# Eight edge counts of the next graph's near mask half, placed at other steps of the attention slot

## The reference

```python
h = jnp.maximum(_layernorm(x), 0.0)
x = x + _L0_gnn_ref(adj, h, W, b)      # max over the first 25 neighbours, then relu(concat(h, agg) @ W + b)
h = jnp.maximum(_layernorm(x), 0.0)
x = x + _L1_gnn_ref(h, adj, ...)       # attention, then feed-forward, each with residual and layer norm

# inside _L1_gnn_ref
allowed = (adj > 0) | (jnp.swapaxes(adj, 1, 2) > 0) | eye
scores = jnp.einsum('bhqd,bhkd->bhqk', q * scale, k)        # 8 heads of 16
scores = jnp.where(allowed[:, None], scores, -jnp.inf)
ctx = jnp.einsum('bhqk,bhkd->bhqd', softmax(scores), v)
```

## Time and profile before

| | |
|---|---|
| median of 3 runs | 1314.69 us (1313.65 to 1317.1) |
| profiled execution, span from first to last instruction | 1313.1 us |
| TensorE matmul busy | 1054.3 us, 80% |
| VectorE busy | 786.5 us, 60% |
| ScalarE busy | 806.3 us, 61% |
| GpSimd busy | 727.8 us, 55% |
| exponentials L1317, 512 instructions | 496.4 us busy, 284.5 us idle before them, 280.0 of it for scores |
| mean granted TensorE clock | 0.945 |

### The profile page before, as it was taken

The page is one execution under the profiler, slowest core; times in us unless marked ns, Lnnn a source line. Parts: engine busy times, 40 slices in busy tenths (PEclk is TensorE's granted clock), DMA queues, the critical chain, the costliest instruction groups (busy, mean ns, idle before and its releaser), DMA issues.

```text
span 1313.1 us, 30142 instructions
## 1 busy us (share of the span) xinstructions
PE 1054.3 (80%) x11425; PEld 454.7 (35%) x11486; DVE 786.5 (60%) x3039; ACT 806.3 (61%) x1032; POOL 727.8 (55%) x743
## 2 busy tenths in 40 slices
PE   0125586169869699999999989998999999989884
PEld 0112341024324243444344334433443334334332
DVE  6866856736766776877686768686245342322323
ACT  1130155057756487778777867787778777866551
POOL 4775755567746567766776677667775750000000
PEclk9997788598989799999999999999999999999997
DMA  6753427335442645364536554643272332000000
GB/s 180 243 132 101 126 74 194 117 92 118 131 127 83 180 106 154 112 179 109 151 116 175 114 150 119 173 109 103 86 145 64 102 111 69 4 17 9 10 8 10
DMA packets 104519, 144.52 MB, mean 110 GB/s; under 512 B 17992, under 2 KB 77136, under 8 KB 104336
## 3 DMA queue, kind: packets, MB, share of 16 engines
q1 hardware_dynamic: 68352, 62.67, 15.6%
q0 software_dynamic: 22816, 44.61, 15.1%
q10 hardware_dynamic: 13168, 34.88, 8.2%
HBM read 124.79 MB, written 12.85 MB: 105 GB/s over the span
## 4 chain that ended last, share of the span: by engine, by line
PE 51%; DVE 20%; ACT 10%; issue 8%; POOL 6%; DMA 3%; DVEq 1%; SPq 0%; ACTq 0%; POOLq 0%
PE sc L1536 15%; PE cb L1556 10%; ACT probs L1317 9%; PE sc L1540 5%; PE m L1613 4%; PE m L1626 4%; DVE agg L912 3%; DVE cand L746 3%; POOL nb_low L638 2%; DVE keys L742 2%; PE m L1438 2%; POOL nb_low L618 2%; DVE st L683 1%; PE sc L1578 1%; PE m L1624 1%
## 5 line engine op out<-in xcount | busy, mean ns | idle before, releaser
L1317 ACT ACTIVATE probs<-sc 128x1024 f32<-128x1024 f32 x512 | 496.4, 1021 | 284.5 <-PE sc L1540 280.0
L618 POOL DMA_INDIRECT nb_low<-h_rows,lsorted x474 | 469.0, 989 | 221.4 <-issue 124.8
L1556 PE MATMUL cb<-probs,va 128*17 128x512 f32 x2048 | 274.1, 608 | 1.8 <-ACT probs L1317 1.1
L912 DVE TENSOR_REDUCE agg<-nb_low 128x128 f32<-128x1024 f32 (+6 forms) x64 | 115.1, 1798 | 102.3 <-DMA nb_low<-h_rows,lsorted 87.3
L1536 PE MATMUL sc<-q_near,k_g 32*128 32x512 f32 x1024 | 149.8, 655 | 25.1 <-ACT probs L1317 21.9
L1536 PE MATMUL sc<-q_far,k_g 32*128 32x512 f32 x1024 | 148.8, 650 | 23.2 <-ACT probs L1317 21.5
L1540 PE MATMUL sc<-barred,negident 32*32 32x512 bf16 x4096 | 112.8, 391 | 0.0
L746 DVE MAX8 cand<-keys 128x8 f16<-128x128 f16 x512 | 105.4, 279 | 2.2
L638 POOL DMA_INDIRECT nb_low<-h_rows,first_lists x80 | 80.0, 1000 | 44.0 <-issue 23.5
L1540 PEld LDWEIGHTS sc<-barred,negident 32*32 32x32 bf16 x4096 | 35.3, 88 | 199.0 <-issue 199.0
L1333 ACT ACTIVATE m<-adj_m 128x1024 bf16<-128x1024 int32 x64 | 67.8, 1059 | 46.7 <-DMA adj_m<-in_adj_dram 46.4
(11 more groups left out here) (186 smaller groups left out, 1506.6 us busy)
## 6 DMA issues: line engine op xcount, KB each, us to landing
adj_t<-in_adj_dram SPq DMA_DIRECT2D x64, 512.0 KB
adj_m<-in_adj_dram ACTq DMA_DIRECT2D x64, 512.0 KB
nb_low<-h_rows,lsorted POOLq DMA_INDIRECT x474
xh<-in_x_dram SPq DMA_DIRECT2D x8, 512.0 KB, 6.5
h_rows<-xh SPq DMA_DIRECT2D x8, 512.0 KB
hl<-h_rows SPq DMA_DIRECT2D x8, 512.0 KB
x<-in_x_dram SPq DMA_DIRECT2D x16, 256.0 KB
out_dram<-h2T SPq DMA_DIRECT2D x16, 256.0 KB
```

The lines of the kernel that those rows point to most:

```text
L618: pool.indirect_dma_start(out=dst, out_offset=None, in_=h_rows[0:(f + 1) * (N + 1), :], in_offset=bass.IndirectOffsetOnAxis(ap=lsorted[:, ...
L912: ch.link(nc.vector.tensor_reduce(a, first.rearrange("p k c -> p c k"), AX.X, ALU.max))
L1317: nc.scalar.activation(probs[:, i % 2, 2 * pair:2 * pair + 2, :], sc[:, 2 * pair:2 * pair + 2, :], ACT.Exp, scale=SCALE).then_inc(s_probs, 1)
L1556: last = nc.tensor.matmul(cb[a * SPAN:a * SPAN + VW, :], va[:, u % 2, a, kt, :], probs[:, i % 2, a, :], start=(kt == 0), stop=(kt == T - 1))
```

## The change

Only the table `NEAR_AT` differs. An entry `n: [(kt, bank), ...]` puts the count of key tile kt, in PSUM bank m[bank], behind the other work of step n on TensorE, and its bar on ScalarE at the same step.

```diff
-NEAR_AT = {17: [(0, 2), (1, 0)], 20: [(2, 2)], 21: [(3, 2)], 23: [(4, 2)], 24: [(5, 2), (6, 0)], 25: [(7, 2)]}
+NEAR_AT = {17: [(0, 2)], 23: [(1, 2), (2, 0)], 24: [(3, 2), (4, 0)], 27: [(5, 2)], 31: [(6, 1), (7, 2)]}
```

## The result

| | before | after |
|---|---|---|
| median of 6 runs, us | 1314.36 (1313.54 to 1317.1) | 1323.4 (1320.15 to 1325.77) |
| ratio | | 1.0071, 95% interval 1.0055 to 1.0087 |
| profiled execution, span, us | 1313.1 | 1324.0 |
| mean granted TensorE clock | 0.945 | 0.942 |

The change makes the kernel 0.7% slower, some 9 us. The forecast was 1321.3 us, in a range of 1313 to 1326.

A forecast was written before the change was run, and what follows sets the result against it. The TensorE-ScalarE loop was taken to bound everything before step 22, VectorE's chain steps 22 to 30 in slots 0 to 4. +2.0 us without the clock and +4.6 for it took 1314.7 to 1321.3 us, range 1313.0 to 1326.0.

The forecast's parts named there:

- Steps 20, 21, 23, 25: Moved counts: -0.36 and -0.49 us in 20 and 21, +0.5 in 23 (slots 0 to 4), -0.30 in 25.
- Step 27: Its count in bank 2 waits for VectorE's late `ctxn`: a 2.6 us stall in slot 4, scores 2.2 us later.
- The slack of `prod`: In step 30, TensorE's 1.00 us wait for `prod` absorbs part of the 2.2 us delay, leaving +1.1 a slot.
- Step 31: Two counts take 0.9 us of TensorE's 1.05 us idle before the next slot's scores: cost 0.
- Slot 1's gain: Step 17 without its second count lets scores 18 and contexts run inside the 11.22 us wait: -4.0 us.
- rival (c): Slot 1: the gain stays out because VectorE's own work bounds what follows; +4.0 us more, 1325.3, chance 0.08.
- The sum without the clock: All slots added with no fall of the clock: +1.3 -2.9 +3.3 +1.1 -0.8 = +2.0 us.
- The clock: TensorE's clock falls behind step 27's stalls: four falls at 1.15 us, +4.6; bounds per fall 0 and 1.8.
- Rival (b): The clock falls in every stalled slot, slot 5 too: with 1.2 us each +9.2, 1323.9 us; chance 0.15.
- Rival (a): The clock holds behind step 27's stalls: only +2.0 us, 1316.7; chance 0.19.
- Rival (d): Step 27's count finds bank 2 free, so the kernel gets faster: -9.5 us, 1305.2; chance 0.06.
- the -0.8 us that the forecast gave slot 6: Slot 6 has no stall: gains of 0.36, 0.49 and 0.30 against +0.35 for count and bar in its step 27.

The follow-up runs named there:

- e1: The changed kernel with the count of key tile 5 at step 25 instead of step 27; 1306.8 us, ratio 0.9944 to the kernel before.
- e3: The kernel before with one count instead of two in step 17 and the others moved up; 1310.3 us, ratio 0.9978.
- e5: The changed kernel with VectorE's `ctxn` ahead of the list tile and second pooling tile; 1306.32 us, ratio 0.9952 to the kernel before.
- e2: The kernel before with only the count of key tile 7 moved from step 25 to step 27, bank 2; 1333.12 us, ratio 1.015.
- e4: The changed kernel with ten unread matmuls ahead of step 27's count (eight in slot 5, none in slot 6); 1317.62 us, ratio 1.0035 to before.
- e6: The kernel before with only the count of key tile 7 moved from step 25 to step 31; 1312.94 us, ratio 1.0001.

## Why the prediction was right

It was right in direction and in mechanism, and short in size: +6.6 us forecast, 9.3 by the ratio. Point by point:

- *Steps 20, 21, 23, 25.* Forecast -0.36, -0.49, +0.5 in slots 0 to 4, -0.30. Measured 3.54 against 3.90 us, 4.53 against 5.02, 4.32 against 3.84 (3.54 in slots 5 and 6), 3.54 against 3.84. All hold. e1 and e3 add what they are worth: 0.8 to 0.9 us a slot for steps 20 and 21 (129.86 against 130.78 in slot 3), and nothing for the second bar of step 23, which lies under VectorE's chain.
- *Step 27.* Forecast a stall of 2.6 us in an ordinary slot, up to 3.6 in others, 1.9 in slot 5, none in slot 6. Measured 2.55 to 2.71 in slots 1, 2 and 4, then 3.57, 3.70, 1.92 and none. e1 (count earlier) and e5 (`ctxn` earlier) take the wait away from either side, and either way the loss is gone; e2 makes it alone, with the old table.
- *The slack of `prod`.* The step said that 1.0 us is absorbed, so that +1.1 a slot remains. With the clock held (e4) slots 2, 3 and 4 take 130.96, 132.04 and 130.97 us against 130.06, 130.78 and 129.66: +0.9, +1.3 and +1.3. Slot 5: forecast +1.1, in e4 +0.9.
- *Step 31.* Forecast 0: 3.54 us in slots 2 to 5, and e6 shows it for one count alone. In slots 0 and 1 it is 3.79 and 3.65 us, in slot 6 4.25 (below). The forecast had no condition on it, and e1's slot 0 shows one: at the low level two counts there cost 1.4 us. In the change no fall met step 31; that was luck of the place.
- *Slot 1's gain.* Forecast -4.0, measured -3.96 at the exponentials of step 19; rival (c), that it stays out, falls. The slot as a whole in e4, without falls of the clock, is 3.2 us shorter than before; the forecast said 2.9.
- *The sum without the clock.* Forecast +2.0. The seven slots of e4's trace add up to 1.5 us more than those of before (+1.1, -3.2, +0.9, +1.3, +1.3, +0.9, -0.7). By the timed ratios it is +4.6 us, with an interval of 2.4 to 6.8, whose lower end lies just above the forecast; whether the clock held in the runs that were not traced, and what the fillers themselves add, stays open.
- *The clock.* This is the term that was too small: the forecast had "four falls at 1.15: +4.6". The runs show five falls, four of them dearer. Steps 20 to 31 of the change take 1.1, 1.6, 1.6, 1.4 and 1.7 us more than those of e4 in slots 0 to 4 (slot 4: 51.33 against 49.60), 7.3 us in all, and e2's two equal stalls differ by 1.6. The bound of 1.8 per fall held. Where it is paid differs from the forecast, which priced a fall by scores to exponentials at 1.2 us and left at most 0.6 for count and projection. In slots 1 to 4 count and projection pay most: from the start of the count to the scores it is 2.68 us in slot 4 (884.35 to 887.03) and 2.82 in slots 1 to 3, against 1.55 in e4's slot 4 (876.24 to 877.79), 1.1 to 1.3 more. The scores pay what is left of the 3.4 us: 1.57 us in slot 4 and 1.43 in slot 2 against 1.14, next to nothing in slots 1 and 3 (1.16 and 1.15). Only slot 0, whose fall began later, pays in the scores (2.09) and the mask (0.65 against 0.43). The difference of the ratios of the change and e4 is 4.7 us, so that the runs give 5 to 7 us for the clock. With 7.3 in place of 4.6 the forecast's own sum is 2.0 + 7.3 = 9.3 us, and the ratio says 0.0071 x 1314.4 = 9.3. That the two agree so closely is partly chance: by the timed ratios the same 9.3 is 4.6 without the clock and 4.7 for it, so that what lies between the two parts is known to some 2 us only.

Rival (b), falls in every stalled slot with slot 5 among them, is wrong in slot 5, where the grant stays at 1.00 behind 1.92 us, though its 1323.9 us lies nearest to the result: its price per fall, 1.2, was too small as well (five falls cost 7.3), and the one fall too many made up for it: 6 x 1.2 = 7.2. That is luck. Slot 5 could have gone the other way, as e6's 1.88 us did. With (b) the prediction named a rule (the Trainium skill, "TensorE: Matmul & The Clock Gate", section "A second HAM failure mode: psum-queue depth-cycling"), that frequent short idles between groups of matmuls, as banks are cycled, make the clock swing. This trace agrees in part only: the clock does fall and recover, but behind single idles of 2.55 us and more, once in a slot, and not behind 1.92.

Rival (a), the clock holds, is what e4 makes true by force; its ratio on the 1314.69 us of the forecast gives 1319.3 against (a)'s 1316.7. Rival (d), the count finds bank 2 free, was put at 1305.2 us; e1 and e5, which bring that about, come to 1307.3 and 1308.4 by their ratios on the same base.

The profile's span of the change is 10.9 us above that of before, more than the 9.3 of the ratio. About 2 us of it is step 12 of slot 0, a wait for other data that takes between 36.9 and 39.8 us in the profiles of these eight kernels, 39.8 in the change and 37.8 before; no part of the table touches it.

## What to carry to other kernels

When instructions are moved in an in-order queue by hand, the bank that each one takes decides more than its own 0.46 us: ask who read that bank last, when that reader ends on *its* engine, and what stands behind the moved instruction. Here a wait that a projection one step later hardly met (0.3 us) came to hold up the count, and behind it projection and scores, by 1.9 to 3.7 us. It shows neither in busy shares nor in the exponentials' idle time, but in the list of waits, and in the one group of the page that stands in the wait. Count a stall of TensorE with what its clock loses behind it (here 1.1 to 1.7 us per stall of 2.55 us or more), and look for the place a little earlier: two steps turned 0.7% slower into 0.6% faster.

## What the runs showed of the hardware

- Idle TensorE and its clock: in the change the grant fell to 0.50 with idles of 2.55, 2.65, 2.71, 3.57 and 3.70 us, and behind 1.92 us it did not. But in e2 two idles of about 3.0 us went one each way, and so did 1.88 us in e6 and 1.90 before, in the same place. Slot 0 fell behind 2.13 us in e1 and behind 1.58 in e5 (window 342.1:345.4, grant 0.50), while e5's waits of 1.3 to 1.6 us in slots 1 to 4 held. So the length of the idle alone doesn't decide between 1.6 and 3.0 us, and the forecast could only be a chance per stall.
- Matmuls whose results nobody reads held the clock at 1.00 through the same waits (e4): ratio 1.0035 against 1.0071, though they do no useful work.
- In the change and in e1 and e5 one instruction in slot 6 is late for no reason that the trace names. In the change, TensorE at the start of slot 7:

```profile
1160.74 0.39 PE L1540 MATMUL sc<-barred,negident 32*32 32x512 bf16 x1
1161.46 0.44 PE L1540 MATMUL sc<-barred,negident 32*32 32x512 bf16 x15 [0.34 <-issue]
```

The second mask matmul comes 0.72 us after the first, where all 16 otherwise follow each other; step 31 of this slot takes 4.25 us there, 4.74 in e1 and 5.03 in e5, and 3.54 in e4, e6 and before. It eats the -0.8 us that the forecast gave slot 6. All three have two counts in step 31, but so has e4, which doesn't show it. It is not the low clock of e1's slot 0: the window 1137.5:1142 of e1 has 1.00. The cause stays open.
